# Attention in 64 units: the first head's probability tiles turned by VectorE in 32x32 blocks and moved between partitions by transfers, value products and output products later in the order

## What is computed

```python
q = query @ W_Query + B_Query          # 8 x 512 x 1024, 16 heads of 64
k = key @ W_Key + B_Key
v = value @ W_Value + B_Value
scores = einsum('bhqd,bhkd->bhqk', q, k) / 8
probs = softmax(scores, axis=-1)       # 512 x 512 for each of 8 x 16 heads
out = einsum('bhqk,bhkd->bqhd', probs, v).reshape(8, 512, 1024)
x = x + out @ W_Output + B_Output
```

## Time and profile before

| | before |
|---|---|
| time, median of 3 runs | 1844.12 us (1844.11 to 1846.59) |
| span of the profiled execution, and its time | 1843.2 us; no time of its own is listed for it; the fastest run shown is 0.9 us above this span |
| TensorE matmul, busy | 1663.1 us, 90% |
| VectorE, busy | 1209.8 us, 66% |
| ScalarE, busy | 843.8 us, 46% |
| GpSimd, busy | 608.1 us, 33% |
| DMA | 109.46 MB, mean 59 GB/s |
| attention stage | from about 437 to 1662 us of the span |

### The profile page before, as it was taken

The page is one execution under the profiler, slowest core; times in us unless marked ns, Lnnn a source line. Parts: engine busy times, 40 slices in busy tenths (PEclk is TensorE's granted clock), DMA queues, the critical chain, the costliest instruction groups (busy, mean ns, idle before and its releaser), DMA issues. The chain is left out here.

```text
span 1843.2 us, 25796 instructions
## 1 busy us (share of the span) xinstructions
PE 1663.1 (90%) x8789; PEld 1128.1 (61%) x8789; DVE 1209.8 (66%) x2689; ACT 843.8 (46%) x1870; POOL 608.1 (33%) x730
## 2 busy tenths in 40 slices
PE   6569999996999999999999999999999999973584
PEld 4447777754666666666666666666666766642352
DVE  6445656532777777776776776776777677757761
ACT  3324343431555555555555555555555555531110
POOL 2143445430333323332332332333232323220375
PEclk9669999997999999999999999999999999985697
DMA  8100000003323232323232322222223223213254
GB/s 254 27 23 12 12 12 1 1 0 106 69 47 69 47 92 46 69 69 69 47 92 47 67 72 61 54 65 74 56 60 79 59 53 86 46 45 99 44 85 58
DMA packets 68961, 109.46 MB, mean 59 GB/s; under 512 B 18400, under 2 KB 50400, under 8 KB 68832
## 3 DMA queue, kind: packets, MB, share of 16 engines
q1 hardware_dynamic: 62688, 99.29, 22.1%
q0 software_dynamic: 6144, 8.52, 3.0%
HBM read 27.84 MB, written 12.85 MB: 22 GB/s over the span
## 5 line engine op out<-in xcount | busy, mean ns | idle before, releaser
L1128 POOL TENSOR_SCALAR at_Pr<-at_Pr,at_rinv 128x512 f32<-128x512 f32 x512 | 355.8, 695 | 841.2 <-DVE at_rinv L1158 841.2
L1093 ACT ACTIVATE at_Pr<-at_ps,at_nmax 128x512 f32<-128x512 f32 x512 | 352.2, 688 | 535.2 <-DVE at_nmax L1153 533.6
L1153 DVE TENSOR_REDUCE at_nmax<-at_ps 128x1 f32<-128x512 f32 x512 | 351.2, 686 | 154.0 <-PE at_ps L958 142.5
L958 PE MATMUL at_ps<-at_k,at_q 128*128 128x512 f32 x1024 | 420.7, 492 | 10.8 <-DMA at_k<-at_k_own 9.1
L969 PE MATMUL at_ps<-k_ident,at_Pr 128*128 128x128 f32 x2048 | 309.8, 274 | 4.5 <-POOL at_Pr L1128 4.5
L969 PEld LDWEIGHTS at_ps<-k_ident,at_Pr 128*128 128x128 f32 x2048 | 250.5, 140 | 90.2 <-POOL at_Pr L1128 27.7
L1165 DVE COPY at_PT<-at_ps 128x512 f32<-128x512 f32 x384 | 261.4, 681 | 0.0
L958 PEld LDWEIGHTS at_ps<-at_k,at_q 128*128 128x128 f32 x1024 | 174.6, 191 | 130.7 <-issue 121.2
L979 PE MATMUL at_ps<-at_PT,at_V 128*64 128x512 f32 x1024 | 235.4, 602 | 0.9 <-DVE at_PT L1165 0.9
L1158 DVE RECIPROCAL at_rinv<-at_rsum 128x1 f32<-128x1 f32 x512 | 83.3, 163 | 161.1 <-ACT at_Pr L1093 159.1
L979 PEld LDWEIGHTS at_ps<-at_PT,at_V 128*64 128x64 f32 x1024 | 68.1, 137 | 122.5 <-issue 121.4
(11 more groups left out here) (236 smaller groups left out, 1996.5 us busy)
## 6 DMA issues: line engine op xcount, KB each, us to landing
at_k<-at_k_own SPq DMA_DIRECT2D x256, 256.0 KB, 4.3
k_x<-in_x SPq DMA_DIRECT2D x8, 512.0 KB, 8.5
mg_ctx<-in_ctx SPq DMA_DIRECT2D x8, 512.0 KB, 8.7
mx_ctxn<-in_ctx SPq DMA_DIRECT2D x8, 512.0 KB, 3.8
rows<-m_ctxT SPq DMA_DIRECT2D x16, 256.0 KB, 2.6
out<-k_x SPq DMA_DIRECT2D x8, 512.0 KB, 3.5
r_w<-in_L_ffn_w SPq DMA_DIRECT2D x16, 256.0 KB, 5.5
mx_w<-in_L_ffn_w SPq DMA_DIRECT2D x2, 1024.0 KB, 10.0
```

What stands on the lines that cost most here:

```text
L958: ins = pe.matmul(ps[:, S_BANK + j % 2, :], q2[:, u % 2, h, q:q + P], k2[:, u % 2, h, part, :], start=part == 0, stop=part == 1)
L1093: act.activation(Pr[:, j % 4, :], ps[:, S_BANK + j % 2, :], ACT.Exp, bias=nmax[:, j % 4:j % 4 + 1], accum_out=rsum[:, j % 4:j % 4 + 1]).th ...
L1128: pool.tensor_scalar(Pr[:, n % 4, :], Pr[:, n % 4, :], rinv[:, n % 4:n % 4 + 1], 1.0, ALU.mult, ALU.mult).then_inc(s["pn"], 1)
L1153: dve.tensor_reduce(nmax[:, j % 4:j % 4 + 1], ps[:, S_BANK + j % 2, :], AX.X, ALU.max, negate=True).then_inc(s["nmax"], 1)
```

## The change

- The tiles of the first head (0 to 3) are no longer turned by TensorE. VectorE turns each in 32x32 blocks from `Pr` into a new buffer `blocks` (`turn_blocks`, steps 2 to 5). Then SyncE issues 16 transfers, each of 32 partitions x 2 KB (64 KB), from one quarter of the partitions to another, into `PT0` (`move_blocks`). `blocks` has two buffers, `PT0` one: the moves of unit u wait for the value products of unit u-1, and the value products of unit u wait for the moves.
- Tiles 4 to 7 go through TensorE as before, into `PT1`; tiles 4 and 5 are now turned in steps 6 and 7 (they were in 6 and 7 before, too), 6 and 7 in steps 0 and 1 of the next iteration. ScalarE still copies 4 and 5, VectorE 6 and 7.
- `project_values(u)` moves to step 2 of iteration u and waits for `ql` of unit u+1, because the queries of u+1 lie in the same bank. The value products of unit u-1 are split in halves, in steps 5 and 6. The output products of unit u-2 stand in steps 3 and 4; their first half now shares `O_BANK` with the value products, which therefore wait for `add_out(u-2, 0)`, in VectorE's step 4.
- VectorE takes `row_sum` after `row_max` in steps 0, 4, 5 and 7 (`AFTER_MAX`). `heads_out` moves to step 7. The loops of TensorE and VectorE run one iteration longer.

```diff
+                def move_blocks(u):
+                    sp.wait_ge(s["blocks"], TPB * (u + 1))
+                    wait_count(sp, s["pv"], u)
+                    for to in range(Q4):
+                        for of in range(Q4):
+                            sp.dma_start(PT0[QW * to:QW * to + QW, of, :, :, :],
+                                         blocks[QW * of:QW * of + QW, u % 2, to, :, :, :]).then_inc(s["moved"], 16)
+
+                copy_keys(0)
+                for u in range(U):
+                    if there(u + 1):
+                        copy_keys(u + 1)
+                    move_blocks(u)
...
                 def project_values(u):
                     b, hp = u // HP, u % HP
-                    pe.wait_ge(s["ql"], u + 1)
+                    pe.wait_ge(s["ql"], min(u + 2, U))
...
-                def weigh_values(u):
-                    wait_turned_copies(pe, u, NBL)
-                    pe.wait_ge(s["V"], u + 1)
-                    wait_count(pe, s["x"], 2 * u)
-                    for t in range(TPB):
+                def weigh_values(u, half):
+                    if half == 0:
+                        pe.wait_ge(s["pt_a"], 2 * u + 2)
+                        pe.wait_ge(s["pt_v"], 2 * u + 2)
+                        pe.wait_ge(s["moved"], 16 * MOVES * (u + 1))
+                        pe.wait_ge(s["V"], u + 1)
+                        wait_count(pe, s["x"], 2 * u - 1)
+                    for t in (2 * half, 2 * half + 1):
...
-                for u in range(U + 1):
+                for u in range(U + 2):
                     for j in range(NBL):
                         if there(u):
                             score(u, j)
-                            if j >= 2:
-                                turn(u, j - 2)
                         if j < 2 and there(u - 1):
                             turn(u - 1, NBL - 2 + j)
                         if j < 2 and there(u + 1):
                             project(u + 1, j)
-                        if j == 2 and there(u - 1):
-                            weigh_values(u - 1)
-                        if j == 4 and there(u + 1):
-                            project_values(u + 1)
+                        if j == 2 and there(u):
+                            project_values(u)
+                        if j in (3, 4) and there(u - 2):
+                            output(u - 2, j - 3)
                         if j in (5, 6) and there(u - 1):
-                            output(u - 1, j - 5)
+                            weigh_values(u - 1, j - 5)
+                        if j >= 6 and there(u):
+                            turn(u, j - 2)
...
+                def turn_blocks(u, j):
+                    dve.wait_ge(s["pn"], NBL * u + j + 1)
+                    if j == 0:
+                        wait_count(dve, s["moved"], 16 * MOVES * (u - 1))
+                    dve.transpose(blocks[:, u % 2, :, :, j, :].rearrange("p c t q -> p t c q"),
+                                  Pr[:, j % 4, :].rearrange("p (t c q) -> p t c q", t=TPB, c=Q4)
+                                  ).then_inc(s["blocks"], 1)
...
+                AFTER_MAX = (0, 4, 5, 7)
+                for u in range(U + 2):
                     for j in range(NBL):
+                        if j not in AFTER_MAX:
+                            sum_of_last(u, j)
                         if there(u):
-                            if j >= 1:
-                                row_sum(u, j - 1)
                             row_max(u, j)
-                            if j >= 2:
-                                keep(u, j - 2)
+                        if j in AFTER_MAX:
+                            sum_of_last(u, j)
...
+                        if 2 <= j < 2 + TPB and there(u):
+                            turn_blocks(u, j - 2)
+                        if j in (4, 5) and there(u - 2):
+                            add_out(u - 2, j - 4)
...
-                        if j == 7:
-                            if there(u):
-                                row_sum(u, j)
...
-                                add_out(u - 1, 0)
-                                add_out(u - 1, 1)
```

More of the change, by code:

```diff
@@ L830, in attention @@
     NBL = 2 * TPB
+    Q4 = 4
+    QW = P // Q4
+    MOVES = Q4 * Q4
     with ExitStack() as ctx:
@@ L841, in attention @@
         Pr = sb("Pr", [P, 4, S], F32)
-        PT = sb("PT", [P, 2, 2, TPB, S], F32)
+        blocks = sb("blocks", [P, 2, Q4, TPB, TPB, QW], F32)
+        PT0 = sb("PT0", [P, Q4, TPB, TPB, QW], F32)
+        PT1 = sb("PT1", [P, Q4, TPB, TPB, QW], F32)
         oT = sb("oT", [P, S], F32)
@@ L906, in store_rows, with copy_keys @@
                                  x_all[:, b * TPB:(b + 1) * TPB, :]).then_inc(landed, 16)
-                for u in range(U):
+                def copy_keys(u):
                     sp.wait_ge(s["kh"], u + 1)
@@ L971, in turn @@
                     ins.then_inc(s["t_ps"], 1)
-                def weigh_values(u):
-                    wait_turned_copies(pe, u, NBL)
-                    pe.wait_ge(s["V"], u + 1)
-                    wait_count(pe, s["x"], 2 * u)
-                    for t in range(TPB):
-                        for h in range(2):
+                def weigh_values(u, half):
[6 more added lines that the diff above has]
+                    for t in (2 * half, 2 * half + 1):
+                        for h, turned in ((0, PT0[:, :, t, :, :]), (1, PT1[:, :, t, :, :])):
                             ins = pe.matmul(ps[AD * h:AD * h + AD, O_BANK, :], V[:, u % 2, t, AD * h:AD * h + AD],
-                                            PT[:, u % 2, h, t, :], start=t == 0, stop=t == TPB - 1)
-                    ins.then_inc(s["pv"], 1)
+                                            turned.rearrange("p a j q -> p a (j q)"), start=t == 0, stop=t == TPB - 1)
+                    if half:
+                        ins.then_inc(s["pv"], 1)
                 def output(u, half):
@@ L987, in output @@
                             pe.wait_ge(first["loaded"], 16 * 7)
+                    else:
+                        wait_count(pe, s["x"], 2 * u)
                     for t in (2 * half, 2 * half + 1):
-                        ins = pe.matmul(ps[:, Y_BANK - half, D * (t % 2):D * (t % 2) + D], oT[:, P * t:P * t + P],
+                        ins = pe.matmul(ps[:, O_BANK + half, D * (t % 2):D * (t % 2) + D], oT[:, P * t:P * t + P],
                                         wo_s[:, u % HP, :], start=True, stop=True)
@@ L1084, in _ @@
                 keys(0)
-                values(0)
                 for u in range(U + 1):
                     for j in range(NBL):
-                        if j == 4 and there(u - 1):
-                            heads_out(u - 1)
                         if there(u):
                             act.wait_ge(s["nmax"], NBL * u + j + 1)
-                            wait_count(act, s["t_ps"], NBL * u + j - 3)
+                            if j < TPB:
+                                wait_count(act, s["t_ps"], TPB * (u - 1) + j + 1)
+                            else:
+                                act.wait_ge(s["blocks"], TPB * u + j - TPB + 1)
                             act.activation(Pr[:, j % 4, :], ps[:, S_BANK + j % 2, :], ACT.Exp,
@@ L1106, in _ @@
                                 keys(u + 1)
-                            if j == 5:
-                                values(u + 1)
+                        if j == 3 and there(u):
+                            values(u)
                         if there(u) and j - 2 in ON_ACT:
[L1110 to L1114, removed]
+                            act.wait_ge(s["t_ps"], TPB * u + j - 2 - TPB + 1)
+                            act.copy(turned_rows(j - 2), turned_bank(j - 2)).then_inc(s["pt_a"], 1)
+                        if j == 7 and there(u - 1):
+                            heads_out(u - 1)
                 for k in range(DC):
@@ L1207, in _, with sum_of_last @@
                                   ).then_inc(s["scaled"], 1)
-                for u in range(U + 1):
+                def sum_of_last(u, j):
+                    if j == 0 and there(u - 1):
+                        row_sum(u - 1, NBL - 1)
+                    if j and there(u):
+                        row_sum(u, j - 1)
+                AFTER_MAX = (0, 4, 5, 7)
+                for u in range(U + 2):
                     for j in range(NBL):
+                        if j not in AFTER_MAX:
+                            sum_of_last(u, j)
                         if there(u):
-                            if j >= 1:
-                                row_sum(u, j - 1)
                             row_max(u, j)
-                            if j >= 2:
-                                keep(u, j - 2)
+                        if j in AFTER_MAX:
+                            sum_of_last(u, j)
                         if j < 2 and there(u - 1):
```

44 lines of the change are left out of this document (20 added, 24 removed).

## The result

The changed kernel takes 1889.73 us (median of 4 runs, 1889.20 to 1890.36) against 1844.11 us (4 runs, 1843.48 to 1846.59): 1.0246 times the time before, 95% interval 1.0231 to 1.026. It is 45.6 us slower; the forecast was 21 us slower. The profiled execution has a span of 1887.5 us.

The account below looks back on a forecast made before the run. TensorE's strict list bounds the stage: 15.51 us of work plus 1.22, 0.5, 1.23 and 0.11 makes 18.57 a unit against 18.16, +26 us; router work -8, ends +3: +21, 1865 us. Range 1785 to 1945, likeliest case 1842 to 1890.

Parts of the forecast that it names:

- Wait 1: TensorE before the turn of tile 6, whose reciprocal now follows the maximum of tile 7: 1.22 us a unit.
- Wait 3: TensorE before the first value product, for VectorE's addition to x in the shared bank: 1.23 us a unit.
- Block turn: VectorE's turn of a first-head tile in 32x32 blocks: taken as 0.61 us, like a copy or maximum.
- rival 2: Block turns on VectorE are dear: at 1.22 us each, 74 us more, 1939 us; chance 0.12.
- Moves: SyncE's 16 transfers a unit: 10.5 to 12.6 us to issue and land, hidden by 1.7 us at least.
- rival 3: The moves bind: at 0.90 us an issue the value products wait 2.3 us longer, 2012 us; chance 0.11.
- The once-in-8 work: Router's turns and logits, 3.1 us every 8 units: half falls into the wait before tile 6's turn, -8 us net.
- the forecast's +3: First iterations and end of the attention stage, outside the steady units: together 3 us more.
- sum of a unit: One attention-stage unit: TensorE's 15.51 us of work plus waits and a bare load, 18.57 us against 18.16.
- Wait 2: TensorE before the value projection in step 2, for the next unit's queries: 0.4 to 0.6, taken as 0.5 us.
- An output half: Half of the output products on TensorE, priced at 0.76 us.
- rival 1: The gain comes through, waits shorter than summed: 1788 us without one large wait, 1669 without all; chance 0.20.

## Why the prediction was right and where it failed

**Right.** Sign and mechanism. TensorE loses 2.24 us of turns and meets waits in strict order that take them back.

- Wait 1: the sum had 2.46 us from score 7 to the turn of tile 6, the trace 2.44. Wait 3: 2.91 from score 4 to the first value product, 2.94.
- Block turn: 0.61 from start to start taken, 0.61 measured, so rival 2 falls. The estimate from the Trainium skill, "VectorE: DVE Perf Modes", The three transpose paths, was 0.71 us for the length of one, against copies of 0.68. The trace agrees on the length, 0.696, but not on the 4 us that it was to add, since the next instruction starts as early behind a block turn as behind a copy.
- Moves: hidden, so rival 3 falls for this order. The 16 took 10.05 us to issue and 12.05 to land, not rival 3's 16.6 or 15.2. An issue at 0.63 stood at the lower edge of the 0.63 to 0.75 named; they were hidden all the same, since they landed in 2.0 and not in 4.3.
- The once-in-8 work: the stores of batches are 153.25 us apart in two rows of SyncE,

```profile
1012.51 1.12 SPq L908 DMA_DIRECT2D rows<-m_ctxT  x2
...
1165.76 1.84 SPq L908 DMA_DIRECT2D rows<-m_ctxT  x2
```

and over six such periods (705.33 to 1627.14) 153.64, that is 8 x 18.96 and 2.0, where the forecast's -8 us made 3.1 into 2.1. The rest outside the periods, 45.6 - 8 x (153.64 - 148.39) = 3.6 us, is near the forecast's +3; its parts were not measured one by one.

**What failed is the sum of a unit**, 18.57 us, against 18.96; 0.39 x 64 = 25 us is the whole difference between 21 and 45.6. That 1889.7 us still lies within 1842 to 1890, by 0.3 us, is luck: the sum stood at 1865. By stretches:

| stretch, load to load | sum had | trace |
|---|---|---|
| score 7 to turn of tile 6 | 2.54 | 2.44 |
| turn of tile 6 | 0.39 | 0.39 |
| query projection to value projection | 5.18 | 5.38 |
| value projection to score 3 | 1.79 | 1.78 |
| score 3 to first value product | 4.01 | 4.16 |
| first value product to score 7 | 4.66 | 4.81 |

("Sum had" spreads the 15.51 us over the rows of before less the turns removed, and adds the waits.) Three terms were mis-sized:

1. *"TensorE's work becomes 17.75 - 2.24 = 15.51 us."* It counted the turns removed but priced the split of the value products at nothing. A second end of 64-column products costs 0.31 us: 4.81 against 4.50 in one piece, and 0.32 in the mean over all units in the kernel before. The row that showed it was there, 0.81 of idle loader at the start of score 3 in the earlier trace rows. Another 0.16 that the sum had too much in this stretch hid part of it; in it are the 0.11 for a bare first load, where the first value product starts 0.03 behind its load (1074.38 and 1074.41).
2. *Wait 2*, "0.4 to 0.6, taken as 0.5", is 0.70: value projection 5.38 behind the query projection, of which 4.68 is TensorE's own. Of the 0.20 missing, 0.09 is the cover of the first loads that the 0.5 allowed for (5.27 - 4.68 is 0.59), which did not come. The other 0.11 is VectorE's chain, 5.38 and not 5.27, most of it since the queries start 0.71 behind the copy of tile 7 (1066.16 and 1066.87) and not 0.61.
3. *An output half* at 0.76: behind a score instead of a turn it is 0.87 (1070.57 to 1071.44). 0.11 in the half that does not lie inside wait 3.

With 0.03 more in wait 3, these are 0.65. Against them stand 0.16 as said and 0.10 between score 7 and the turn. The split was tested by runs; the other two terms are read from the rows alone.

A price of rival 1 was wrong too: it put the absence of one large wait at 64 x 1.2 = 77 us. The two runs that took out one wait each gave 54 and 55.

## What to carry to other kernels

An engine that runs a strict list gets time back from removed work only where no wait follows: place every wait of the new order by its chain, from start to start. Price a moved or split group from the rows on both its sides, and ask which chain runs beside it: the same split cost 14 us and gained 25. Fix the order last and together: the change alone is 2.5% slower; with VectorE's reciprocal, additions and queries placed earlier and block turns and value projection a step later it is 4.5% faster than before.

## What was not expected of the hardware

- 1.2 us of idle time before an instruction was worth 0.84 to 1.02 us a unit when the wait was removed. Part of it is not the wait's: 0.37 us stands before a first 64-column load behind a score in any case, and a turn takes 0.39 us right after a wait but 0.56 behind other work (1055.68 to 1056.24 without wait 1).
- The first full-width load after 64-column products starts 0.81 to 0.82 us after the last of these has ended, in every kernel here, before the last units of the stage. Why it isn't loaded ahead was not settled.
- A transfer of 64 KB between partitions (32 rows of 2 KB) takes 0.63 us of issue, one of 256 KB 0.80 (3.19 / 4; in the earlier trace rows 0.90): a quarter of the bytes, four fifths of the time.
